# GpSimd's two products of a selective scan made for two states at a time instead of four

## What is computed

```python
dt = softplus(dt_in * dt_w[:, 0] + dt_b)
A = -exp(A_log)
dA = exp(dt[..., None] * A)                              # 512 channels x 16 states
x_scaled = (xb * dt)[..., None] * Bp[..., None, :]
_, h = associative_scan(comb, (dA, x_scaled), axis=1)    # h[t] = dA[t] * h[t-1] + x_scaled[t]
y = einsum('bldn,bln->bld', h, Cp) + xb * D_param
y = layernorm(y) * ln_g + ln_b
y = y * silu(z)
out = einsum('bld,ed->ble', y, out_w)
```

## Time and profile before

| What | Value |
|---|---|
| median of 3 runs | 5296.42 us |
| lowest and highest run | 5291.37, 5298.24 us |
| the profiled execution, span from first to last instruction | 5291.6 us |
| PE matmuls busy | 4820.6 us (91%) |
| POOL busy | 4452.7 us (84%), 3336 instructions |
| ACT busy | 3911.0 us (74%) |
| DVE busy | 3739.1 us (71%) |
| mean granted clock of TensorE | 0.967 |

### The profile page before, as it was taken

The page is one execution under the profiler, slowest core; times in us unless marked ns, Lnnn a source line. Parts: engine busy times, 40 slices in busy tenths (PEclk is TensorE's granted clock), DMA queues, the critical chain, the costliest instruction groups (busy, mean ns, idle before and its releaser), DMA issues. The chain is left out here.

```text
span 5291.6 us, 96290 instructions
## 1 busy us (share of the span) xinstructions
PE 4820.6 (91%) x33664; PEld 4234.3 (80%) x33664; DVE 3739.1 (71%) x7504; ACT 3911.0 (74%) x9282; POOL 4452.7 (84%) x3336
## 2 busy tenths in 40 slices
PE   4789999999999999999999999999999999999986
PEld 4678888888888888888888888888888888888776
DVE  3567777777777777777777777777777777777653
ACT  4687787787777787777777777787777777777751
POOL 4998898898898898898888888898898898898840
PEclk8899999999999999999999999999999999999986
DMA  4222222222222222222222222222222322322200
GB/s 96 60 54 71 57 61 72 57 62 72 61 61 68 59 66 66 64 63 64 67 60 64 68 59 64 67 61 64 71 59 61 71 59 61 75 58 58 66 16 25
DMA packets 730625, 329.04 MB, mean 62 GB/s; under 512 B 631542, under 2 KB 655392, under 8 KB 729888
## 3 DMA queue, kind: packets, MB, share of 16 engines
q1 hardware_dynamic: 730144, 322.89, 25.0%
HBM read 307.88 MB, written 14.90 MB: 61 GB/s over the span
## 5 line engine op out<-in xcount | busy, mean ns | idle before, releaser
L1105 DVE TENSOR_TENSOR_SCAN X<-dA,X 128x392 f32<-128x392 f32 x2048 | 1871.4, 955 | 844.9 <-POOL X L474 447.9
L474 POOL TENSOR_TENSOR X<-u,Bb 128x784 f32<-128x784 f32 x1024 | 1898.2, 1854 | 3.9 <-DMA Bb<-proj_rows 3.9
L484 POOL TENSOR_TENSOR X<-X,Cb 128x784 f32<-128x784 f32 x1024 | 1897.2, 1853 | 1.1 <-DVE X L1105 1.1
L907 ACT ACTIVATE dA<-dt,negA 128x195 f32<-128x195 f32 x4096 | 1511.6, 417 | 135.2 <-DVE X L1105 116.2
L601 PE MATMUL YB<-idn,X 128*98 128x128 f32 x8192 | 1106.7, 281 | 25.6 <-POOL X L484 25.4
L601 PEld LDWEIGHTS YB<-idn,X 128*98 128x98 f32 x8192 | 931.3, 132 | 62.9 <-POOL X L484 33.9
L721 PE MATMUL G<-hg,we 128*128 128x196 f32 x4096 | 727.8, 334 | 27.1 <-DVE hg L1221 27.1
L721 PEld LDWEIGHTS G<-hg,we 128*128 128x128 f32 x4096 | 694.9, 194 | 47.4 <-issue 40.8
L578 PE MATMUL SB<-hT,win 128*128 128x196 f32 x2048 | 375.3, 337 | 58.0 <-ACT pT L986 55.8
L548 PE MATMUL YB<-win,idn 128*98 128x196 f32 x2176 | 424.1, 335 | 0.0
L693 PEld LDWEIGHTS G<-vs,pT 98*98 98x98 f32 x4096 | 392.6, 171 | 36.2 <-issue 33.4
(11 more groups left out here) (149 smaller groups left out, 7609.0 us busy)
## 6 DMA issues: line engine op xcount, KB each, us to landing
Bb<-proj_rows SPq DMA_DIRECT2D x256, 392.0 KB, 5.2
Cb<-proj_rows SPq DMA_DIRECT2D x256, 392.0 KB, 4.1
Gb<-gate_rows SPq DMA_DIRECT2D x64, 784.0 KB, 5.5
px<-in_x SPq DMA_DIRECT2D x1024, 36.8 KB
out<-ob SPq DMA_DIRECT2D x64, 196.0 KB
dtin<-proj_rows SPq DMA_DIRECT2D x64, 98.0 KB, 2.8
we<-in_w_e SPq DMA_DIRECT2D x1, 2048.0 KB
proj_rows<-pj SPq DMA_DIRECT2D x64, 25.3 KB
```

What stands on the lines that cost most here:

```text
L474: tt(X[(GROUPS * s + g) % RING][:], u[q % 2][:, c:c + 1, :].broadcast_to([P, NG, T]), Bb[:, NG * ng:NG * (ng + 1), :], ALU.mult).then_inc( ...
L484: tt(t[:], t[:], Cb[:, n0:n0 + NG, :], ALU.mult).then_inc(prod_ready, 1)
L907: last = go(dA[i % DRING][:, j, 1:T], dt_[q % 2][:, c, 1:T], ACT.Exp, scale=negA[:, c, n:n + 1])
L1105: v.tensor_tensor_scan(t, dA[i % DRING].rearrange("p n t -> p (n t)"), t, 0.0, ALU.mult, ALU.add).then_inc(scan_done, 1)
```

## The change

Each of the two products of a group is made by two instructions of 2 states (392 elements a partition) in place of one of 4. `xs_pool` and `prod_ready` count pairs of states, so every wait on them is rewritten: each scan waits for its own pair, each half of `times_c` for its own scan, and PE's matmuls of states 0 and 1 for the first half alone.

```diff
@@ SP
-                            after(sp, xs_pool, GROUPS * s - GC + ng + 1)
+                            after(sp, xs_pool, 2 * (GROUPS * s - GC + ng + 1))
...
-                            after(sp, prod_ready, GROUPS * s - GC + ng + 1)
+                            after(sp, prod_ready, 2 * (GROUPS * s - GC + ng + 1))
@@ POOL
-                after(pool, xs_pool, GROUPS * (s - 1))
+                after(pool, xs_pool, 2 * GROUPS * (s - 1))
...
                 after(pool, prod_used, GROUPS * s + g + 1 - RING)
-                tt(X[(GROUPS * s + g) % RING][:], u[q % 2][:, c:c + 1, :].broadcast_to([P, NG, T]), Bb[:, NG * ng:NG * (ng + 1), :],
-                   ALU.mult).then_inc(xs_pool, 1)
+                for h in range(2):
+                    n0 = NG * ng + HALF * h
+                    tt(X[(GROUPS * s + g) % RING][:, HALF * h:HALF * (h + 1), :],
+                       u[q % 2][:, c:c + 1, :].broadcast_to([P, HALF, T]), Bb[:, n0:n0 + HALF, :],
+                       ALU.mult).then_inc(xs_pool, 1)
 
             def times_c(s, g):
 
-                pool.wait_ge(scan_done, 2 * (GROUPS * s + g + 1))
                 if g < GC:
                     pool.wait_ge(C_landed[g], 16 * (s + 1))
-                t = X[(GROUPS * s + g) % RING]
-                n0 = NG * (g % GC)
-                tt(t[:], t[:], Cb[:, n0:n0 + NG, :], ALU.mult).then_inc(prod_ready, 1)
+                for h in range(2):
+                    pool.wait_ge(scan_done, 2 * (GROUPS * s + g) + h + 1)
+                    t = X[(GROUPS * s + g) % RING][:, HALF * h:HALF * (h + 1), :]
+                    n0 = NG * (g % GC) + HALF * h
+                    tt(t, t, Cb[:, n0:n0 + HALF, :], ALU.mult).then_inc(prod_ready, 1)
@@ PE
-                pe.wait_ge(prod_ready, GROUPS * s + g + 1)
                 for j in range(NG):
+                    if j % HALF == 0:
+                        pe.wait_ge(prod_ready, 2 * (GROUPS * s + g) + j // HALF + 1)
                     for k in range(BLK):
@@ DVE
-                dve.wait_ge(xs_pool, GROUPS * s + g + 1)
                 for h in range(2):
                     i = 2 * (GROUPS * s + g) + h
+                    dve.wait_ge(xs_pool, i + 1)
                     dve.wait_ge(dA_ready, i + 1)
```

## The result

| What | Before | After |
|---|---|---|
| median (lowest to highest run) | 5296.39 us (5291.37 to 5298.24) | 5460.10 us (5457.51 to 5464.63) |
| span of the profiled execution | 5291.6 us | 5458.2 us |
| mean granted clock of TensorE | 0.967 | 0.963 |

The changed kernel is slower: ratio 1.0311, 95% interval 1.0297 to 1.0326. The forecast was 5489 us in a range of 5330 to 5590. The span grew by 166.6 us; the forecast had 193. Before and after have 4 runs each in this comparison.

The account below looks back on a forecast made before the run. The prediction took a loop through POOL's gapless stretch from ka to y3 as the bound. On 5296.4 us it added 160 for that stretch, 26 for the clock and 7 for the ends: 5489 us, range 5330 to 5590.

Parts of the forecast that it names:

- The price of a half: POOL's products: 392 elements cost 0.98 us from start to start, so each split adds 0.146 us.
- The first rival: POOL between ka and y3: small instructions are cheap and the kernel gets faster, 5277 us; chance 0.15.
- The loop: ka, gapless POOL, y3, output projection, tanh, gate_x, scores, next ka: its length is the step, 40.75 us of it POOL.
- ka to y3: POOL's stretch without idle rows: 17 splits make it 2.5 us a step longer, 160 us over 64 steps.
- The second rival: Output projection: y3 doesn't hold PE; growth arrives over scan, taps and tanh, 0.6 us a step, 5335 us; chance 0.08.
- The second half of the step: POOL outside ka to y3: 15 splits, 2.2 us, lie in its gaps and make nothing late; costed at nothing.
- The finer waits: Added waits on PE's matmuls and DVE's second scans: costed at nothing, 6 us if their cover is gone.
- The clock: PE's new idle time ahead of the output projection adds half-clock time, 0.41 us a step, 26 us in all.
- the third rival: From the output projection on: the new gap brings half clock in every step, 104 us, 5567 us; chance 0.10.
- The ends: First three steps grow by 4.7 instead of 2.5 us, 7 us more; the drain has no products.
- the forecast's own range: Whole run: 5400 us (split at 0.09 us) to 5590 us (0.20 us, half the steps with a slow stretch).

Follow-up runs that it names:

- e11: The kernel before with ka multiplied by a constant weight tensor in place of by itself; 5293.64 us, ratio 1.0002.
- e2: The changed kernel with only the 17 products from ka to y3 split, the other 15 whole; 5461.49 us, ratio 1.0316.
- e4: The changed kernel without POOL's y3 multiplication, its semaphore still counted up at the same place; 5398.08 us, ratio 1.0196.
- e1: The changed kernel with only the 15 products outside the stretch from ka to y3 split; 5276.37 us, ratio 0.9966.
- e9: The changed kernel with only the inputs of groups 0, 1, 14 and 15 split; 5277.93 us, ratio 0.9963.
- e3: The changed kernel with all products whole again but its finer waits kept; 5294.83 us, ratio 1.0001.
- e5: The changed kernel with 4 more unread filler matmuls ahead of the first scores (7 in place of 3); 5466.77 us, ratio 1.0320.
- e10: The kernel before (whole products) with the key square moved from POOL to DVE and 4 more unread matmuls ahead of the scores; 5247.10 us, ratio 0.9909.
- e12: e10 with the inputs of groups 0, 1, 14 and 15 split; 5255.71 us, ratio 0.9921.
- e8: e1 with 4 more unread filler matmuls ahead of the first scores; 5261.82 us, ratio 0.9937.

## Why the prediction was right, step by step

**The price of a half: right.** The line through 784 and 2 elements gave 0.98 us; measured 0.975 (half of 1.95). A split costs 2 x 0.975 - 1.81 = 0.14 us where 0.146 was forecast. ka's 0.80 us spoke against it, and the argument that ka is cheap because it reads one tensor twice holds (e11). The Trainium skill, "GPSIMD Engine Reference", section "Performance versus the Vector engine", gives an operation on two tensors about 2.6 cycles an element at 1.2 GHz and calls that the floor of its two time-shared reads. The trace agrees for two tensors: the line through 784 and 2 elements has 2.12 ns an element, an estimate of 2.5 such cycles. It doesn't for ka, whose 840 ns in all lie under the 849 that the page's figures would make of 392 elements, also an estimate; there the measurement decides. Why one tensor read twice is cheaper, no run here shows. The first rival, small instructions that are cheap, is out.

**The loop: right.** ka to y3 without an idle row, 43.12 us where 43.2 was forecast, L627 with 133.0 us of listed waits (less than the 150 forecast) at 2.28 us in the step shown, the wait ahead of ka 0.51 us where 0.6 was forecast. e2 shows that the inner halves make the loss, e4 that without y3's product the projection doesn't wait. The second rival, that y3 isn't what holds PE, would have given 0.6 us a step by the prediction (its own figures, 1.5 us late less 0.99 of slack, make it 0.5); that path was measured at 0.42 (e4).

**The second half of the step: costed at nothing, in fact -0.17 us.** The gain of the earlier inputs of groups 0, 1, 14 and 15 (e1, e9) was overlooked. The forecast looked for gains only behind ka, where POOL is late anyway.

**The finer waits: nothing, as forecast** (e3).

**The clock: nearly the right sum, for the wrong reason.** The new idle time did fall ahead of L622 (2.28 us). The step that failed is that the clock would fall behind it. The half clock came behind the old gap at the scores, and in nearly every step, as the third rival said of the new gap; but there it costs 0.96 us and not 1.62. The 1.62 was read from a window that isn't a step: 1539.45:1619.82 holds 533 matmuls where a step has 529. Its length is that of the step ahead of it, its clock that of the next. From ka to ka these two are:

```profile
1460.87:1541.24 80.37, 77.29 (x529) 68.72 (x528) 58.27 (x117) 60.96 (x146) 69.58 (x52) 0.94 0.27 63
1541.24:1620.91 79.67, 74.59 (x529) 65.67 (x528) 58.30 (x117) 60.93 (x146) 69.54 (x52) 0.98 0.27 63
```

The 80.37 us go with a granted clock of 0.94, half clock at both places. A step at 0.98, with the fall at the scores alone, took 79.67, that is 0.93 more than 78.74, much as in the changed kernel. So 104 us was too high a price for a fall in every step. The mean step over the undisturbed one was 79.15 - 78.74 = 0.41 us before and is 81.93 - 80.97 = 0.96 now: 0.55 us more a step, where 0.41 was added. That the two come near each other is luck, as the 0.41 was only the old cost taken once more. Why the clock falls in so many more steps is open.

**The ends: too much.** Forecast were 64 steps at full growth and 7 us more. 56 steps grew in full. What lies outside them grew by 166.6 - 56 x (81.93 - 79.15) = 11 us, of which 7.6 stand ahead of the first ka (208.05 to 215.63); the forecast gave the 8 other steps 20 us and added 7. This is the term that was mis-sized most. The upper end of the forecast's own range is off as well: 0.20 us a split, half the steps with a slow stretch and 7 us add up to some 5573 us, not 5590; nothing else hangs on it.

The terms side by side, on the span:

| Term | Forecast | Measured |
|---|---|---|
| ka to y3 | 64 x 2.5 = 160 | 56 x 2.40 = 134 |
| earlier inputs, second half | 0 | 56 x -0.17 = -10 |
| clock | 26 | 56 x 0.55 = 31 |
| the rest of the run | 7 | 11 |
| sum | 193 | 166 |

## What to carry to other kernels

An engine at 84% can be the bound of every step: look for a stretch without an idle row whose end somebody starts within a tenth of a microsecond, and cost a split by how many of its instructions lie in that stretch. Price an instruction by a row that reads as many tensors, not only by one of its size. Split where the engine has slack and a consumer waits for the first half, and leave whole what stands in the dense stretch: the four splits of e9 gained 0.4%, the seventeen of e2 lost 3.2%.

## What the runs showed of the hardware that was not expected

POOL's product of a tensor with itself is 18% cheaper than with another of the same size: 840 against 1019 ns for 392 elements a partition.

The half clock of TensorE doesn't simply follow the longest gap. In the changed kernel PE stands for 2.28 us ahead of the projection and runs at full clock behind it; it stands for 1.65 us ahead of the scores, and the clock falls there. Fill that gap, and it falls behind the other (e5). The Trainium skill, "TensorE: Matmul & The Clock Gate", Part 1, ties the half clock to idle time of the array. The runs agree that it comes behind gaps (1.65 us in the changed kernel, 2.30 in e5); which of two gaps it follows can't be read from their lengths here.

In these runs the clock also evened out small differences. e2, the changed kernel and e5 have undisturbed steps of 81.14, 80.97 and 80.96 us, and parts at half clock in 47, 55 and 33 of 56 steps at two different places; their mean steps are 81.92, 81.93 and 81.92. With e10 and e12 it is 78.20 and 78.06 undisturbed, and 78.51 and 78.52 in the mean. In the changed kernel the slow part stands some 56 us after ka in step after step, so the step and the clock's falls keep time with each other. Why they settle at just these lengths was not tried. What follows for a measurement is that 0.1 to 0.2 us saved in such a step need not show at all until the half clock is out of it, as it is in e8.
